# Attention output of a gated block: normalised in channel layout, with the sums spread by a selection matrix and the mask applied on GpSimd

## What is computed

```python
dot = jnp.einsum('bhdt,bhds->bhts', q, k) / math.sqrt(HEAD_DIM)
mask = target_mask[:, :, :, None] * source_mask[:, :, None, :]
dot = mask * dot - (1.0 - mask) * NEG
amap = jax.nn.softmax(dot, axis=-1) * mask
out = jnp.einsum('bhts,bhds->bhdt', amap, v)
...
x = x + jnp.tanh(g_xattn[0]) * xattn(layernorm(x), ctx, mask, mask, Wq, bq, Wk, bk, Wv, bv)
x = x + jnp.tanh(g_ffn[0]) * ffn(layernorm(x), W1, W2)
```

## Time and profile before

| | before |
|---|---|
| median of 3 runs | 226.73 us (226.59 to 228.67) |
| the profiled execution | 227.11 us, of which the span is 225.6 us |
| PE busy | 176.1 us (78%) |
| DVE busy | 135.4 us (60%) |
| ACT busy | 119.2 us (53%) |
| POOL busy | 93.1 us (41%) |

### The profile page before, as it was taken

The page is one execution under the profiler, slowest core; times in us unless marked ns, Lnnn a source line. Parts: engine busy times, 40 slices in busy tenths (PEclk is TensorE's granted clock), DMA queues, the critical chain, the costliest instruction groups (busy, mean ns, idle before and its releaser), DMA issues.

```text
span 225.6 us, 4985 instructions
## 1 busy us (share of the span) xinstructions
PE 176.1 (78%) x1922; PEld 101.0 (45%) x1934; DVE 135.4 (60%) x264; ACT 119.2 (53%) x167; POOL 93.1 (41%) x165
## 2 busy tenths in 40 slices
PE   1578589889896997897999969979988899953513
PEld 0445434355464453554555435546554555522111
DVE  2457924656875693679686846887785635171310
ACT  2325134887977756463665555646645574721301
POOL 8634893200356227203853480057008204617250
PEclk9999857999999999999999999999999999995555
DMA  5484651200000022000010230000000000000000
GB/s 144 90 266 155 201 209 40 53 6 4 0 6 17 4 47 51 0 4 0 4 17 17 47 87 23 4 0 4 23 4 1 21 8 3 0 23 4 25 0 23
DMA packets 8055, 9.23 MB, mean 41 GB/s; under 512 B 1420, under 2 KB 6732, under 8 KB 8028
## 3 DMA queue, kind: packets, MB, share of 16 engines
q1 hardware_dynamic: 7080, 8.45, 13.3%
q10 hardware_dynamic: 952, 0.46, 0.8%
HBM read 5.66 MB, written 1.05 MB: 30 GB/s over the span
## 4 chain that ended last, share of the span: by engine, by line
PE 50%; DVE 19%; POOL 11%; ACT 8%; issue 6%; DMA 4%; POOLq 1%; ACTq 0%; DVEq 0%
PE ps_exp L932 22%; PE ps_pv L948 8%; DVE nmx L699 7%; ACT probs L536 4%; PE ps_max L1010 3%; PE ps_exp L994 3%; DVE hb L746 2%; PE ps_max L925 2%; DVE hs L751 2%; POOL y L382 2%; DMA brow<-in_L_xattn_bq 2%; POOL hq L409 2%; PE ps_exp L822 2%; ACT hb L585 2%; DMA q<-negm 2%
## 5 line engine op out<-in xcount | busy, mean ns | idle before, releaser
L699 DVE TENSOR_REDUCE nmx<-ps_max 128x2 f32<-128x512 f32 x122 | 78.3, 684 | 35.2 <-PE ps_max L925 34.9
L536 ACT ACTIVATE probs<-ps_exp 128x1024 f32<-128x1024 f32 x64 | 65.5, 1023 | 52.7 <-PE ps_exp L932 52.3
L932 PE MATMUL ps_exp<-q,k 32*128 32x256 f32 x512 | 74.7, 409 | 17.3 <-DVE nmx L699 13.0
L925 PE MATMUL ps_max<-k,q 32*128 32x256 f32 x488 | 71.4, 410 | 0.6 <-DVE q L641 0.4
L932 PEld LDWEIGHTS ps_exp<-q,k 32*128 32x128 f32 x512 | 46.7, 189 | 39.8 <-issue 24.3
L925 PEld LDWEIGHTS ps_max<-k,q 32*128 32x128 f32 x488 | 43.2, 190 | 1.2 <-issue 0.8
L948 PE MATMUL ps_pv<-probs,v_aug 128*32 128x256 f32 x512 | 41.3, 395 | 0.0
L403 POOL TENSOR_SCALAR hs<-hs,ys 128x1 f32<-128x1 f32 x8 | 3.0, 375 | 59.8 <-DVE hs L751 59.8
L948 PEld LDWEIGHTS ps_pv<-probs,v_aug 128*32 128x32 f32 x512 | 10.1, 108 | 21.4 <-issue 21.0
L746 DVE SCALAR_TENSOR_TENSOR hb<-hb,ps_exp 128x512 f32<-128x512 f32 x16 | 11.0, 686 | 12.7 <-ACT hb L585 12.7
L376 POOL TENSOR_TENSOR qk<-qk,mask_b 128x512 f32<-128x512 f32 (+1 forms) x8 | 9.1, 1137 | 18.7 <-ACT qk L501 18.7
(11 more groups left out here) (133 smaller groups left out, 230.2 us busy)
## 6 DMA issues: line engine op xcount, KB each, us to landing
w_nat<-in_L_ffn_W SPq DMA_DIRECT2D x2, 1024.0 KB, 6.9
out<-x_sb SPq DMA_DIRECT2D x8, 128.0 KB, 1.7
c_sb<-in_ctx SPq DMA_DIRECT2D x3, 256.0 KB, 8.8
mask_b<-in_mask_Bx1x_fk SPq DMA_DIRECT2D x1, 768.0 KB, 7.7
k<-qk SPq DMA_DIRECT2D x12, 64.0 KB
q<-qk SPq DMA_DIRECT2D x12, 64.0 KB
x_sb<-in_x SPq DMA_DIRECT2D x1, 512.0 KB, 8.6
x_sb<-in_x SPq DMA_DIRECT2D x2, 128.0 KB, 3.3
```

The costliest lines, as they stand in the source:

```text
L536: nc.scalar.activation(probs[:, s % PROBS, :], ps_exp[:, exp_at[("exp", s)] % 2, :], ACT.Exp).then_inc(S["exp_done"], 1)
L699: nc.vector.tensor_reduce(max_columns(g, hh), ps_max[:, at % VEC, :].rearrange("t (c s) -> t c s", c=DC), AX_X, ALU.max, negate=True).then ...
L925: return nc.tensor.matmul(bank[:, c * T:(c + 1) * T], at_rows(q4, b, h)[:, c * 128:(c + 1) * 128], at_rows(k4, b, h), start=True, stop=True)
L932: return nc.tensor.matmul(bank[:, o:o + T], at_rows(k4, b, h)[:, c * 128:(c + 1) * 128], at_rows(q4, b, h), start=True, stop=True)
```

## The change

`gather_heads` now loads `sel` as the stationary operand and streams the attention output through it, so that the result has channels on the partitions and positions in the columns. `sel` gets a second half in which the row with a head's sum is spread to all 8 channels of the head: 4 matmuls of 64x256 instead of 4 of 128x72. The target mask is multiplied on by POOL (`mask_targets`, a new event in step 9, 128x512 from `pv_sb` into the new tile `pv_m`); channels are gathered from `pv_m`, sums from the unmasked `pv_sb`. The gather moves from step 10 to step 11, and DVE's part of steps 10 and 11 becomes one piece in step 11: reciprocal of 128x256 sums, product, addition to `x_sb`, statistics. `turn_back`, the event `back` and its bank are gone.

```diff
-        ENTRY_EVENTS = {"att": 10, "back": 11, "y_max": 13, ...
+        ENTRY_EVENTS = {"mask_t": 9, "att": 11, "y_max": 13, ...
...
-            vec_order += [u for u in events(s) if u[0] in ("v", "w_total", "att", "back", "down")]
+            vec_order += [u for u in events(s) if u[0] in ("v", "w_total", "att", "down")]
...
-                v = sel[:, HP * HD:O_COLS].rearrange("p (i j) -> p i j", i=2)
+                v = sel[:, GROUP:2 * GROUP].rearrange("p (i j d) -> p i j d", i=2, j=4)
                 nc.gpsimd.affine_select(out=v, in_=v, compare_op=ALU.not_equal, fill=1.0, base=-HD,
-                                        pattern=[[-16, 2], [-32, 4]], channel_multiplier=1).then_inc(S["consts"], 1)
+                                        pattern=[[-16, 2], [-32, 4], [0, HD]], channel_multiplier=1).then_inc(S["consts"], 1)
...
+            def mask_targets(b):
+
+                pool.wait_ge(S["pv_copied"], 2 * (b + 1))
+                if b:
+                    pool.wait_ge(S["vec_full"], vec_at[("att", b - 1)] + 1)
+                nc.gpsimd.tensor_tensor(pv_m[:], pv_sb[:], mask_b[:, b, :].unsqueeze(1).to_broadcast([128, 2, T]),
+                                        ALU.mult).then_inc(S["pv_masked"], 1)
...
             def attention_out(b):
 
                 at = vec_at[("att", b)]
-                o_ps = ps_max[:, at % VEC, 0:2 * DC * O_COLS].rearrange("t (i n) -> t i n", i=2 * DC)
                 dve.wait_ge(S["vec_full"], at + 1)
-                link(nc.vector.reciprocal(rec[:], o_ps[:, :, HP * HD:O_COLS]))
-                r = rec[:].rearrange("t (c f) h -> t c (f h)", c=DC)
-                link(nc.vector.tensor_tensor(r, r, mask_t[:, b, :].unsqueeze(2).to_broadcast([128, DC, H]), ALU.mult))
-                nc.vector.tensor_tensor(attT[:].rearrange("t (i h d) -> t i h d", i=2 * DC, h=HP),
-                                        o_ps[:, :, 0:HP * HD].rearrange("t i (h d) -> t i h d", h=HP),
-                                        rec[:].unsqueeze(3).to_broadcast([128, 2 * DC, HP, HD]),
-                                        ALU.mult).then_inc(S["vec_out"], 1)
-
-            def add_attention(b):
-                at = vec_at[("back", b)]
-                dve.wait_ge(S["vec_full"], at + 1)
-                nc.vector.tensor_tensor(x_sb[:, b, :], x_sb[:, b, :], ps_max[:, at % VEC, 0:T], ALU.add).then_inc(S["vec_out"], 1)
+                link(nc.vector.reciprocal(attT[:], ps_max[:, at % VEC, T:2 * T]))
+                nc.vector.tensor_tensor(attT[:], ps_max[:, at % VEC, 0:T], attT[:], ALU.mult).then_inc(S["vec_out"], 1)
                 dve.wait_ge(S["vec_out"], at + 1)
+                link(nc.vector.tensor_tensor(x_sb[:, b, :], x_sb[:, b, :], attT[:], ALU.add))
                 link(nc.vector.bn_stats(stats2[:], x_sb[:, b, :]))
                 nc.vector.bn_aggr(mv2[:], stats2[:]).then_inc(S["ln2_stats"], 1)
...
             def gather_heads(b):
+
                 bank = take_vec(("att", b))
                 pe.wait_ge(S["consts"], 7)
-                pe.wait_ge(S["pv_copied"], 2 * (b + 1))
-                for i in range(2 * DC):
-                    c, f = i // 2, i % 2
-                    ins = nc.tensor.matmul(bank[:, i * O_COLS:(i + 1) * O_COLS], pv_sb[:, f, c * 128:(c + 1) * 128], sel[:],
-                                           start=True, stop=True)
-                ins.then_inc(S["vec_full"], 1)
-
-            def turn_back(b):
-                bank = take_vec(("back", b))
-                pe.wait_ge(S["vec_out"], vec_at[("att", b)] + 1)
-                for c in range(DC):
-                    ins = nc.tensor.transpose(bank[:, c * 128:(c + 1) * 128], attT[:, c * 128:(c + 1) * 128], ident[:])
+                pe.wait_ge(S["pv_masked"], b + 1)
+                for of, o in ((pv_m, 0), (pv_sb, 1)):
+                    for f in range(2):
+                        ins = nc.tensor.matmul(bank[GROUP * f:GROUP * (f + 1), o * T:(o + 1) * T], sel[:, GROUP * o:GROUP * (o + 1)],
+                                               of[:, f, :], start=True, stop=True)
                 ins.then_inc(S["vec_full"], 1)
```

More of the change, by code:

```diff
@@ L38, in gated_block @@
     V_LEN = 2 * DC * H * VH
-    O_COLS = (HP + 1) * HD
+    GROUP = HP * HD
     with ExitStack() as ctx:
@@ L79, in gated_block @@
         ones = sb("ones", [128, 128], F32)
-        sel = sb("sel", [128, O_COLS], F32)
+        sel = sb("sel", [128, 2 * GROUP], F32)
         q4 = sb("q4", [128, 2, QH, 2 * T], F32)
@@ L92, in gated_block @@
         pv_sb = sb("pv_sb", [128, 2, T], F32)
+        pv_m = sb("pv_m", [128, 2, T], F32)
         stats = sb("stats", [128, 2, 6], F32)
@@ L99, in gated_block @@
         negm = sb("negm", [HP, T], F32)
-        rec = sb("rec", [128, 2 * DC, HP], F32)
         attT = sb("attT", [128, T], F32)
@@ L127, in gated_block @@
             vec_full vec_out amax_out mix_out exp_full exp_done
-            shift_in pv_done pv_copied
+            shift_in pv_done pv_copied pv_masked
             ln2_stats y_ready y_max y_scale yq_ready tanh_done up_out h_max h_scale hq_ready stored
@@ L145, in gated_block @@
         HALF_EVENTS = {"shift": 4 - AHEAD}
-        ENTRY_EVENTS = {"att": 10, "back": 11, "y_max": 13, "y_quant": 13, "y_turn": 15, "upa": 16, "ha": 16, "ra": 17,
+        ENTRY_EVENTS = {"mask_t": 9, "att": 11, "y_max": 13, "y_quant": 13, "y_turn": 15, "upa": 16, "ha": 16, "ra": 17,
                         "upb": 18, "hb": 18, "rb": 19, "h_quant": 19, "h_turn": 21, "down": 23}
@@ L428, in _ @@
                         mask_v(i)
-                    if what == "back":
+                    if what == "mask_t":
+                        mask_targets(i)
+                    if what == "att":
                         normalise_y(i)
@@ L784, in _ @@
                         attention_out(i)
-                    if what == "back":
-                        add_attention(i)
                     if what == "y_max":
@@ L1065, in _ @@
                         gather_heads(i)
-                    if what == "back":
-                        turn_back(i)
                     if what == "y_turn":
```

## The result

The changed kernel takes 242.59 us (median of 4, 241.23 to 246.85), against 226.7 for the kernel before: 1.0656 times as long, 95% interval 1.0597 to 1.0714; that ratio leaves out the slowest of the four executions, which fell into a slower state of the chip (the median of the other three is 241.34 us). The direction was forecast, the size was not: some +15 us where the sum gave +4.95. In the profiled executions the span went from 225.6 to 242.3 us, +16.7, and the mean granted TensorE clock from 0.929 to 0.893 of full speed.

A forecast was written before the change was run, and what follows sets the result against it. The prediction took DVE's queue to bound steps 10 to 13 of an entry, with PE mostly setting the pace elsewhere. Its terms summed to +4.95 us, giving a forecast of 231.6 us, range 228.4 to 234.8.

The forecast's parts named there:

- The forecast's own terms: Costs in us: entries 2 and 4 2.7, entry 0 1.7, 1 and 3 0.6, 5 1.0, 6 -0.2, tail -0.85.
- the rival at 2.25 us: DVE's reciprocal takes eight cycles a column, 2.25 us: +2.95 on the forecast, 234.6 us; chance 0.12.
- the gather's two halves side by side: On PE, the gather's 64-column halves run side by side in about 0.95 us; one after the other about 1.7.
- one of the prediction's own signs of being wrong: The prediction is wrong if the gather waits for POOL's mask, then 1.27 us more; the mask was costed at nothing.
- The slack behind `y` in entries 1 and 3: Step 13 comes 1.85 to 2.0 us later, but slack behind `y` swallows all except 0.3 us per entry.
- Addition and statistics stay: In DVE's work per entry, addition and statistics were taken as unchanged, within a net lengthening of 1.34 us.
- the delay of step 13 one for one: DVE work ahead of step 12's first row maximum delays step 13 equally: 1.34 us later in entries 2 and 4.
- their total over 18 us instead of 13.0: Expected sign: PE's waits for row maxima total over 18 us, up 1.3 or more in step 13 of entries 0, 2, 4, 5.
- the cheap reciprocal: DVE's reciprocal costs as much as any pass, 0.4 us: 2.2 us faster, 224.5 us; chance 0.05.
- The pay in full of the turning back: PE gains 8 x 0.4 us of work and 3.8 us of waiting: -7, about 220 us; chance 0.03.
- the lag caught up: Slack behind step 13 halves four costs of 1.0 to 1.7 us: about +2.2, or 228.9 us; chance 0.17.
- halves that don't overlap: On PE the gather's halves run in turn, ending 0.75 us later: +1.5 to +2, or 233.4 us; chance 0.1.

The follow-up runs named there:

- e5: Changed kernel with five unused matmuls behind step 12 of entries 0 to 5 and the product written back to PSUM before the addition; 234.21 us.
- e2: Changed kernel with five unused matmuls filling TensorE's pause behind step 12's scores in entries 0 to 5; 236.94 us.
- e4: Kernel before with one unused 128x256 reciprocal added on DVE in step 11, old gather kept; 239.12 us.
- e9: Both kernels unchanged, profiled again twice each; before 228.07 and 228.33 us, changed 243.17 and 244.42 us.
- e3: Changed kernel with the product written back to its PSUM bank, so the addition reads one operand from PSUM; 239.01 us.
- e1: Changed kernel with its reciprocal cut to 32 of 256 columns, leaving most sums undivided; 224.97 us.
- e7: Kernel before with the gather in step 11 instead of 10 and the turning back in 12 instead of 11; 224.03 us.
- e6: Changed kernel with sums sent by DMA to 128x32 for a short reciprocal and back, the gather moved to step 12; 239.94 us.
- e8: Changed kernel with its gather and normalisation in step 10 instead of 11; 256.14 us.

## Why the prediction was right in direction and wrong in size

The 16.7 us of the profiled execution come apart as follows, each from the table:

- **The forecast's own terms, +4.95, stand.** Entry 0 1.62 for 1.7; with the clock held and the addition short (e5) 0.36, 1.30, 0.37, 1.31, 1.00, -0.21 for 0.3, 1.35, 0.3, 1.35, 1.0, -0.2, and -0.74 for -0.85. Behind them: a reciprocal of 1.754 us for 1.8 (so the rival at 2.25 us fell, and with it the estimate of 2.1 us plus a fixed part from the Trainium skill's "VectorE: DVE Perf Modes", section "First, the fixed hardware budget"); the gather's two halves side by side, from 57.17 to 58.25 in entry 0, 1.08 us for 0.95; the mask hidden, but for the tail: there the gather waited 1.41 us for it, one of the prediction's own signs of being wrong, but the reciprocal, behind `rb` anyway, only 0.15. The slack behind `y` in entries 1 and 3 swallowed the rest as said: step 13 of entry 1 was 2.00 us late in e5, the end of the entry 0.36.
- **The clock, +8.25, had no term.** Entries 1 to 5: 1.13 + 1.54 + 1.27 + 1.56 + 1.20 = 6.7 (after less e2), and step 17's 1.54. In entry 2 both kernels begin step 13 2.00 us late against the entry's start; the 1.54 arise behind it. Shown by e2, e4 and e9. Of these, step 17's can come to the kernel before as well.
- **The addition, +2.1 and some 0.4 in the tail, was mis-sized.** "Addition and statistics stay": the instruction stayed, but its second input moved from PSUM to SBUF, and POOL's `hq` fell beside it. 0.7 in each of entries 2, 4 and 5 (e2 less e5), 0.43 in the tail.
- **The start, +0.95**, lies before the first use of anything changed; the repetitions of before differ there by -0.8 to +1.3. It is not the change's.

4.95 + 8.25 + 2.1 + 0.4 + 0.95 = 16.65.

The step that failed is the one that priced the delay of step 13 one for one and said that elsewhere PE mostly sets the pace. It looked at when step 13 starts and not at how long PE stands ahead of it, and so put at nothing what the pause costs PE behind it; the runs showed 8.25 us there, half of the 16.7. The pieces were all there: step 13 later by 1.34, the wait of 0.79 ahead of step 12 gone, the turning back's 0.41 and PE's 0.05 ahead of it gone, and 0.46 left. Against them, the gather (1.08) now stands behind step 11's scores, and these begin only 0.77 sooner. They add up to 1.34 + 0.79 + 0.41 + 0.05 + 0.46 - 0.31 = 2.74 us; e3, with the short addition, shows 2.72, and the 0.7 of the longer addition makes the 3.41 of the changed kernel. The prediction said "their total over 18 us instead of 13.0" (it was 23.6) but did not ask what a pause does to an engine whose clock is granted.

Of the rivals, the cheap reciprocal gave its own terms part by part when it was made true in e1. The pay in full of the turning back, the lag caught up, and halves that don't overlap did not occur; the 3.8 us that the first of these took for PE's waiting are of its weight loads; PE itself waited 1.6 us there, once, in the tail. None of the rivals had the clock in it.

**What stays open.** What decides which pause of 2.0 to 3.4 us is followed by a stretch: the same pause in the same kernel is, in one execution, and is not, in another; where in time it falls differs between them, but the runs were not made to show what matters in it. Nor was it tried whether e7's order gains from filled pauses in the tail, where the clock is low over the last 20 us or more in all kernels.

## What to carry to other kernels

When a change makes another engine late, price two things for TensorE: how much later its work starts, and how long it stands in one piece; here a pause of up to 1.6 us cost itself alone, one of 2.5 to 3.4 us in most cases 1.1 to 1.6 us more behind it. Splitting the late engine's work around a deadline (e7) gained where gathering it in one place lost. When an operand moves from PSUM to SBUF, look at what GpSimd does in that moment.

## What the runs showed of the hardware

- **Half clock behind a pause.** Pauses between steps 8 and 56 of 1.6 us and less (before, e1, e2, e6, e8) were followed by no stretch; of 1.82 (e8) in 1 of 2; of 1.96 ahead of step 16 in 9 of 14 profiles; of 2.07 (e4) in 3 of 6 entries; of 2.48 in 5 of 6 over the three profiles of the changed kernel (entries 1 and 3), but in neither of e3's two; of 2.7 in all three of e3's entries 2, 4 and 5, but in one of four in entry 0 (changed kernel, e3); of 2.77 (e8) in 1 of 3; of 3.41 in 8 of 9 (entries 2, 4 and 5). Single pauses of 2.27 and 3.23 in e6 and of 2.47 in e8 each had one. A stretch of 3.4 us begins between 0.2 us before and 1.6 us after work has resumed and costs 1.1 to 1.6 us. The four of 6.8 us there (e6, e8, both repetitions of the changed kernel) began in the pause itself, 0.5 to 1.3 us before its end; in the changed kernel they cost 2.5 and 3.2 us. The Trainium skill warns of idle gaps of TensorE in "TensorE: Matmul & The Clock Gate", section "HAM oscillation — how this bites in real kernels"; the traces agree in kind, but the pauses here that were followed by a stretch were for the most part shorter than the gaps it warns of.
- **VectorE beside GpSimd.** A 128x256 addition with two SBUF inputs took 0.42 us alone and up to 1.12 beside a GpSimd instruction of 1.12 us; with one input in PSUM 0.42 beside the same instruction. "GPSIMD Engine Reference" of the Trainium skill, section "Specifications", states that the two engines share SBUF interfaces, with contention when a VectorE instruction has two SBUF inputs; the traces agree, and give the price: the addition ended 0.27 us behind the other, whenever it had begun.
- **The reciprocal** costs 154, 352 and 1754 ns for 2, 32 and 256 columns: 6.3 ns for each further column from 32 on, five times that of a row maximum.
- **Weight halves.** The gather's four matmuls of 256 f32 columns into two 64-column halves (two records each, eight of some 0.39 us) took 1.08 us in all; one pair, a matmul in either half, spans 0.65, the other 0.60.
